# Weighing the heads' values ahead of the next query and key projection in an attention step

## The chip, the core and the metric

The kernel runs on one core of a Trainium2 chip. The metric is the device time of one execution in microseconds (us); lower is better. The core has five engines with a queue each: TensorE (PE, with its weight loads shown apart as PEld), VectorE (DVE), ScalarE (ACT), GpSimd (POOL) and SyncE (SP), which here only issues transfers. Each works through its queue in order and meets the others by semaphores.

## What is computed

A decoder layer on x of 8 x 256 x 256 in float32: causal self-attention with 16 heads of 64, a normalisation, three rounds of a slot attention with a GRU cell against a context of 120 rows, a normalisation, and a mixture of 8 experts of which each token takes 2, with a shared expert, and a last normalisation. The change lies in the first part alone:

```python
q = (x @ Wq).reshape(N, S, HEADS, HEAD_DIM).transpose(0, 2, 1, 3)
k = (x @ Wk).reshape(N, S, HEADS, HEAD_DIM).transpose(0, 2, 1, 3)
v = (x @ Wv).reshape(N, S, HEADS, HEAD_DIM).transpose(0, 2, 1, 3)
logits = jnp.einsum('nhid,nhjd->nhij', q, k) * scale
causal = 1000000000.0 * (jnp.tril(jnp.ones((S, S), dtype=logits.dtype)) - 1.0)
logits = logits + causal[None, None, :, :]
attn = jax.nn.softmax(logits, axis=-1)
out = jnp.einsum('nhij,nhjd->nhid', attn, v)
out = out.transpose(0, 2, 1, 3).reshape(N, S, HEADS * HEAD_DIM)
return out @ Wo + bo
...
x = _layernorm(x + _L0_attn_ref(x, ...), axis=-1)
x = _layernorm(x + _L0_xattn_ref(x, ctx_1024, ...), axis=-1)
x = _layernorm(x + _L0_ffn_ref(x, ...), axis=-1)
```

## The kernel before

The attention works on 64 items. An item is one batch (of 8) and one pair of heads (of 8). Since every matrix of a projection is held as two float16 parts, high and low, a projected tile is three products for each of two chunks of the model dimension (`split_matmuls`, L31): six matmuls for the queries and six for the keys of an item.

The items are software-pipelined over the loop `for j in range(FIRST, LAST + 1)`, which stands once in the program of each engine, written out by hand. What TensorE does in step j, in this order: `turn_prob(j - 1)` transposes the probabilities of item j-1 (L589), `scores(j + 1)` makes the scores of the two heads (L618, each head on one half of the array's rows, into banks 2 and 3), `project_qk(j + 2)` projects queries and keys (L31, tiles `wqkv` and `xT`, into bank 0), and `weigh_values(j - 1)` multiplies the turned probabilities with the values (L628, each head on one half of the array's columns, into the last quarter of banks 4 and 5). Then follows, in odd steps, `project_v(j + 1)` (L31), and in even steps from 4 on a share of the output projection (L31, tiles `wo` and `oT`). In many steps there are also transposes of a later input (L578), preparations for the next stage (`prep_tensor`), or transposes of finished rows.

The other engines in step j:

- ScalarE copies the second head's turned probabilities out of PSUM (L738), makes the high half of a piece of the experts' weights (L477), the first head's exponentials of item j+1 (L721), the queries of j+2 (L728), the high half of the heads of j-1 (`heads_high`, L745), the keys of j+2 (L731), the second head's exponentials, and in early steps high halves of attention weights (L711).
- VectorE copies the first head's turned probabilities (L823), makes the reciprocal sums (L816), low halves of weight pieces (L487), masks and maxima of the scores of j+1 (L809), values out of PSUM (L835), the low half of the heads of j-1 (`heads_low`, L829), and behind that, by step, a batch's output with its statistics (L844, L848, L853, L855), the low half of an input (L787), low halves of attention weights (L796), and more pieces (L487).
- GpSimd multiplies the probabilities by the reciprocal sums (L542).

The waits that matter: `turn_prob(m)` waits for the normalised probabilities and for both halves of the heads of item m-1, since they share a bank. `weigh_values(m)` waits for both copies of the turned probabilities (`pT_out`) and for the values. `project_qk(n)` and `scores(n - 1)` wait for the queries and keys of item n-1 to be out of bank 0. Each bank and each tile `pT` exists once, so that the copies of item m also wait for the weighing of m-1.

SyncE streams the experts' weights in, in pieces, and their split halves out to memory, as VectorE gets done with them.

Of the kernel before, what the change touches and what calls it, by code (L numbers as in the profile page):

```python
# [34 lines left out]
def decoder_layer(nc, a, out):  # L35
# [9 lines left out]
    ITEMS = NB * PAIRS  # L45
# [11 lines left out]
    with top:  # L57
# [256 lines left out]
        def vw_bank(i):  # L314
            return 6 if i == 0 else i - 1 if i < VW_EARLY else i % 4

        def vw_tensor(i):

            b, k = i // 2, i % 2
            before = [q for q in range(i) if vw_bank(q) == vw_bank(i)]  # L320
            if before:
                PE.wait_ge(vw_lo, before[-1] + 1)
            elif i == 0:
                PE.wait_ge(h_out, SHARES_MADE - KEYS)
            elif i == 1:
                PE.wait_ge(qk_out, 2 * ITEMS)
            elif i == 2:
                PE.wait_ge(v_out, ITEMS // 2)
            else:
                PE.wait_ge(masked, 4 * ITEMS)  # L330
            for r in range(DC):
                mm = PE.matmul(ps[0:M, vw_bank(i), 0:3 * P], pnT[:, r, b * M:(b + 1) * M],
                               wb[:, r, k * 3 * P:(k + 1) * 3 * P], start=r == 0, stop=r == DC - 1)
            mm.then_inc(vw_mm, 1)
# [16 lines left out]
        with ExitStack() as c:  # L351
# [57 lines left out]
            def output_share(j):  # L409

                m = j - 4
                return (m // PAIRS, m % PAIRS) if m >= 0 and m % 2 == 0 else None
# [6 lines left out]
            def batch_turned(j):  # L419

                return j // PAIRS + X_EARLY if j % PAIRS == 3 and j // PAIRS + X_EARLY < NB else None
# [4 lines left out]
            def share_at(j):  # L426

                n = (j - 16) // 2
                return n if j % 2 == 0 and 0 <= n < SHARES_MADE else None
# [138 lines left out]
            def attention_tensor():  # L568
# [13 lines left out]
                def turn_prob(m):  # L582
                    PE.wait_ge(normed, 4 * (m + 1))
                    if m >= 1:
                        PE.wait_ge(o_hi, m)
                        PE.wait_ge(o_lo, m)
                    for h in range(2):
                        for blk in range(3):
                            mm = PE.transpose(ps[:, 4 + h, blk * P:blk * P + P],  # L589
                                              prob[m % 3][:, h, blk * P:blk * P + P], ident[:, :])  # L590
                    mm.then_inc(p_turned, 1)

                def project_qk(n):
                    b, cols = n // PAIRS, slice(n % PAIRS * P, n % PAIRS * P + P)
                    if n >= 1:
                        PE.wait_ge(qk_out, 2 * n)
                    if n % PAIRS == 0:
                        PE.wait_ge(x_hi, b + 1)
                        PE.wait_ge(x_lo, b + 1)
                    for k in range(2):  # L600
                        if n == 0:
                            PE.wait_ge(w_lo, k + 1)
                        if n == PAIRS // 2:
                            PE.wait_ge(w_lo, k + 4)
                        w = [[wqkv[h][:, ch, k, cols] for h in range(2)] for ch in range(DC)]
                        x = [[batch_xT(h, b)[:, ch, :] for h in range(2)] for ch in range(DC)]
                        mm = split_matmuls(PE, ps[:, 0, k * S:(k + 1) * S], list(zip(w, x)))
                    mm.then_inc(qk_mm, 1)

                def scores(m):  # L610

                    PE.wait_ge(qk_out, 2 * (m + 1))
                    if m >= 1:
                        PE.wait_ge(masked, 4 * m)
                    for t in range(2):
                        for h in range(2):
                            r = slice(HD * h, HD * h + HD)
                            mm = PE.matmul(ps[:, 2 + h, query_tile(t)], qk[m % 2][r, 0, t * P:t * P + P],  # L618
                                           qk[m % 2][r, 1, 0:(t + 1) * P], start=True, stop=True)
                    mm.then_inc(s_mm, 1)  # L620

                def weigh_values(m):
                    PE.wait_ge(pT_out, 2 * (m + 1))
                    PE.wait_ge(v_out, m // 2 + 1)
                    for t, key, at in ((0, 0, 0), (1, 0, P), (1, 1, 2 * P)):
                        for h in range(2):
                            r = slice(HD * h, HD * h + HD)
                            mm = PE.matmul(ps[r, 4 + t, 384:512], v_sb[m // 2 % 2][:, key, m % 2, r],  # L628
                                           pT[:, h, at:at + P], start=key == 0, stop=key == t, skip_group_check=True)
                    mm.then_inc(o_mm, 1)  # L630

                def project_v(n):

                    b, cols = n // PAIRS, slice(n % PAIRS * P, n % PAIRS * P + 2 * P)
                    if n == 0:
                        PE.wait_ge(w_lo, 3)
                    else:
                        PE.wait_ge(v_out, n // 2)
                    if n == PAIRS // 2:
                        PE.wait_ge(w_lo, 6)  # L640
                    for t in range(S // P):
                        x = [[batch_xT(h, b)[:, ch, t * P:t * P + P] for h in range(2)] for ch in range(DC)]
                        w = [[wqkv[h][:, ch, 2, cols] for h in range(2)] for ch in range(DC)]
                        mm = split_matmuls(PE, ps[:, 1, t * 2 * P:(t + 1) * 2 * P], list(zip(x, w)))
                    mm.then_inc(v_mm, 1)

                def output_projection(b, slot):
                    PE.wait_ge(o_lo, b * PAIRS + slot + 2)
                    PE.wait_ge(o_hi, b * PAIRS + slot + 2)
                    if b == 0:  # L650
                        PE.wait_ge(w_lo, 7 + slot // 2)
                    if b == 0 and slot == 0:
                        PE.wait_ge(x_hi, 1)
                        PE.wait_ge(x_lo, 1)
                    elif b >= 1 and slot == 0:
                        PE.wait_ge(y_added, b)
                    for t in range(2):
                        o = [[oT[h][:, s, t * P:t * P + P] for h in range(2)] for s in (slot, slot + 1)]
                        w = [[wo[h][:, s, :] for h in range(2)] for s in (slot, slot + 1)]
                        mm = split_matmuls(PE, ps[:, 7, t * D:t * D + D], list(zip(o, w)), first=slot == 0 and t == 0,  # L660
                                           last=slot == PAIRS - 2, skip_group_check=True)
                    mm.then_inc(y_mm, 1)
# [4 lines left out]
                for j in range(FIRST, LAST + 1):  # L667
                    if 0 <= j - 1 < ITEMS:
                        turn_prob(j - 1)
                    if 0 <= j + 1 < ITEMS:  # L670
                        scores(j + 1)
                    if j == ITEMS:
                        vw_tensor(1)
                    if j + 2 < ITEMS:
                        project_qk(j + 2)
                    if 0 <= j - 1 < ITEMS:
                        weigh_values(j - 1)
                    if j + 1 < ITEMS and j % 2 == 1:
                        project_v(j + 1)
                    if j == ITEMS - 1:  # L680
                        vw_tensor(0)
                    if output_share(j) is not None:
                        output_projection(*output_share(j))
                    if share_at(j) is not None:
                        turned = min(X_EARLY + (j + 4) // PAIRS, NB)
                        PE.wait_ge(x_hi, turned)
                        PE.wait_ge(x_lo, turned)
                        prep_tensor(share_at(j))
                    if batch_turned(j) is not None:
                        PE.wait_ge(x_hi, batch_turned(j))  # L690
                        PE.wait_ge(x_lo, batch_turned(j))
                        turn_inputs(batch_turned(j))
# [226 lines left out]
            constants_vector()  # L919
            attention_vector()  # L920
            attention_tensor()
            attention_pool()
            nc.all_engine_barrier()
# [1548 lines left out]
```

## Time and profile before

| | us |
|---|---|
| median of 3 runs | 920.73 |
| lowest and highest run | 920.72, 922.23 |
| profiled execution | 920.84 |
| span of the core in it | 919.60 |

| engine | busy us | share of the span | instructions |
|---|---|---|---|
| PE | 888.7 | 97% | 8158 |
| PEld | 674.2 | 73% | 8158 |
| DVE | 637.2 | 69% | 1823 |
| ACT | 551.8 | 60% | 1337 |
| POOL | 348.7 | 38% | 485 |

A matmul's duration in the trace includes the time in which it drains beside the next one. So what a group of matmuls costs is read from its start to the start of the next group, and not from its busy time. The rows of a timeline merge instructions of a kind that follow each other (x12); the time behind the start is that of the merged group. What stands in brackets at the end of a row is the time that the engine sat idle before it, and who ended that.

### The profile page before, as it was taken

Reading aid. Unit: us, or ns where it says so; the run is one execution under the profiler, and the core shown is the slowest. Engines: PE = TensorE matmul, PEld = TensorE weight load, DVE = VectorE, ACT = ScalarE, POOL = GpSimd, SP = SyncE. Lnnn points to the kernel's source line nnn. Section 1 sums busy time; section 2 is a strip of 40 time slices with the busy share of each in tenths; the row PEclk is TensorE's granted clock in tenths of the full one; section 3 lists DMA queues with packets and bytes.
Section 4 is the critical chain, followed back from the end, with each engine's and each line's share of the span. In section 5 each row is a group of like instructions: output and inputs, shape, how many; then the busy total and the mean of one; then the engine's idle time right before and its main releaser. Section 6 shows DMA issues by size and latency. Waiting matters only on the chain. (4 is left out here: it accounts for less than half of the span.)

```text
span 919.6 us, 23720 instructions
## 1 busy us (share of the span) xinstructions
PE 888.7 (97%) x8158; PEld 674.2 (73%) x8158; DVE 637.2 (69%) x1823; ACT 551.8 (60%) x1337; POOL 348.7 (38%) x485
## 2 busy tenths in 40 slices
PE   5999999999999999899999999999999999999996
PEld 4777778777777777666666666676788888887864
DVE  4667777776677766557676777778867767776755
ACT  5778776776676776446555554555455555554555
POOL 2333433342333333224344342444624444444423
PEclk9999999999999999999999999999999999999998
DMA  9743424343324230310000000089542222332226
GB/s 321 186 139 108 161 101 139 111 149 100 125 72 138 93 134 29 44 56 1 1 1 1 2 1 1 1 312 402 173 125 50 51 48 44 51 50 48 43 30 189
DMA packets 61585, 88.09 MB, mean 96 GB/s; under 512 B 17280, under 2 KB 46528, under 8 KB 61344
## 3 DMA queue, kind: packets, MB, share of 16 engines
q1 hardware_dynamic: 53439, 75.52, 24.8%
q0 software_dynamic: 7488, 10.27, 6.9%
q8 instruction: 72, 1.18, 0.5%
q10 hardware_dynamic: 544, 0.79, 0.3%
q14 instruction: 42, 0.34, 0.1%
HBM read 56.00 MB, written 30.56 MB: 94 GB/s over the span
## 5 line engine op out<-in xcount | busy, mean ns | idle before, releaser
L2153 PE MATMUL ps<-slots,e 128*128 128x128 f16 x1872 | 190.1, 219 | 2.1 <-DVE xs L2320 1.9
L542 POOL TENSOR_SCALAR prob<-prob,rden 128x128 f32<-128x128 f32 (+1 forms) x256 | 108.0, 438 | 213.9 <-DVE rden L816 213.9
L2153 PEld LDWEIGHTS ps<-slots,e 128*128 x1872 | 152.5, 97 | 35.7 <-issue 5.0
L721 ACT ACTIVATE prob<-prob,nmx 128x128 f32<-128x128 f32 (+1 forms) x256 | 114.1, 450 | 40.8 <-DVE nmx L809 38.0
L2161 PE MATMUL ps<-e,xT 128*128 x312 | 117.3, 378 | 0.0
L2250 ACT ACTIVATE slots<-slots 128x512 f32<-128x512 f32 x78 | 49.1, 630 | 106.8 <-DVE slots L2304 106.8
L31 PE MATMUL ps<-s,whh 128*128 128x512 f16 x432 | 105.0, 378 | 0.0
L31 PE MATMUL ps<-xT,wqkv 128*128 128x256 f16 x768 | 96.2, 276 | 1.0 <-DVE wqkv L796 1.0
L31 PEld LDWEIGHTS ps<-xT,wqkv 128*128 128x128 f16 x768 | 70.4, 98 | 30.1 <-issue 22.3
L2162 PE MATMUL ps<-e,xT 128*128 x312 | 85.0, 273 | 0.0
L1665 POOL DMA_INDIRECT xg<-rows_x,dst x39 | 40.9, 1049 | 105.5 <-DVE mask L2293 102.1
L809 DVE CUSTOM_DVE_ANT_0 prob<-ps,mask 128x128 f32<-128x128 f32 (+1 forms) x256 | 75.9, 353 | 4.0 <-PE ps L618 4.0
L2309 DVE TENSOR_TENSOR xT<-slots,xT 128x1024 f16<-128x1024 f32 x39 | 47.8, 1225 | 40.0 <-ACT xT L2256 40.0
L2125 POOL DMA_INDIRECT back_y<-xs,dst x39 | 62.2, 1594 | 30.3 <-DMA back_y<-xs,dst 13.4
L2304 DVE SCALAR_TENSOR_TENSOR slots<-ps,b1e 128x512 f32<-128x512 f32 x78 | 53.7, 691 | 26.4 <-PE ps L2153 25.6
L31 PEld LDWEIGHTS ps<-s,whh 128*128 128x128 f16 x432 | 42.2, 101 | 35.5 <-issue 0.2
L823 DVE COPY pT<-ps 128x384 f32<-128x384 f32 x64 | 35.5, 555 | 44.3 <-PE ps L589 44.1
L829 DVE TENSOR_TENSOR oT<-ps,oT 128x256 f16<-128x256 f32 x64 | 27.2, 424 | 51.0 <-ACT oT L745 50.4
L618 PE MATMUL ps<-qk 64*128 64x128 f32 (+1 forms) x512 | 59.3, 350 | 0.7 <-ACT qk L731 0.7
L31 PE MATMUL ps<-an,wqkv 120*128 120x256 f16 x432 | 59.1, 272 | 0.5 <-POOL an L1389 0.5
L31 PEld LDWEIGHTS ps<-an,wqkv 120*128 120x128 f16 x432 | 41.9, 97 | 21.4 <-POOL an L1389 1.0
L1371 POOL TENSOR_TENSOR dl<-slots,nn 128x512 f32<-128x512 f32 x24 | 30.4, 1268 | 70.9 <-ACT nn L1248 70.8
(262 smaller groups left out, 1899.3 us busy)
## 6 DMA issues: line engine op xcount, KB each, us to landing
halves<-parted SPq DMA_DIRECT2D x36, 512.0 KB, 2.9
piece<-in_L_ffn_ew SPq DMA_DIRECT2D x32, 512.0 KB, 4.4
e<-halves SPq DMA_DIRECT2D x16, 1024.0 KB, 15.3
piece<-in_L_ffn_sh_w SPq DMA_DIRECT2D x4, 512.0 KB, 8.8
sw<-halves SPq DMA_DIRECT2D x4, 512.0 KB, 6.3
rows_x<-xs SPq DMA_DIRECT2D x4, 512.0 KB, 6.8
xs<-back_y SPq DMA_DIRECT2D x8, 256.0 KB, 5.2
out<-xs SPq DMA_DIRECT2D x8, 256.0 KB, 2.1
```

The costliest lines, as they stand in the source:

```text
L31: mm = pe.matmul(out, w, x, start=first and n == 0, stop=last and n == len(products) - 1, **kw)
L542: PO.tensor_scalar(prob[m % 3][:, h, r], prob[m % 3][:, h, r], rden[m % 2][:, h, t:t + 1], 1.0, ALU.mult, ALU.mult).then_inc(normed, 1)
L618: mm = PE.matmul(ps[:, 2 + h, query_tile(t)], qk[m % 2][r, 0, t * P:t * P + P], qk[m % 2][r, 1, 0:(t + 1) * P], start=True, stop=True)
L721: SC.activation(p, p, ACT.Exp, bias=nmx[u][:, h, t:t + 1], scale=-1.0, accum_out=den[u][:, h, t:t + 1]).then_inc(exped, 1)
L809: VE.tensor_tensor_reduce(prob[m % 3][:, h, r], ps[:, 2 + h, r], mask[:, r], -1.0, HIGHEST, ALU.add, ALU.min, nmx[m % 2][:, h, t:t + 1]).t ...
L2125: PO.indirect_dma_start(back_y, bass.IndirectOffsetOnAxis(ap=dst[:, i:i + 1], axis=0), yo[i % 2], None, compute_op=ALU.add).then_inc(rows_ ...
L2153: yield PE.matmul(ps[:, 2 * u + q, (k % 4) * P:(k % 4) * P + P], w[ch][h], xgT[u][j][:, ch, :], start=n == 0, stop=n == 3 * DC - 1)
L2161: yield PE.matmul(ps[:, 4 + u, :], he[u][0][:, k, :], w, start=k == 0, stop=False, skip_group_check=True)
L2162: yield PE.matmul(ps[:, 4 + u, 0:D], he[u][1][:, k, :], w[:, 0:D], start=False, stop=k == IC - 1, skip_group_check=True)
L2250: SC.activation(z, z, ACT.Gelu_apprx_tanh).then_inc(U_gelu, 1)
L2304: VE.scalar_tensor_tensor(z, ps[:, 2 * u + q, :].rearrange("p (k t) -> p k t", k=4), 1 / WS, bias, ALU.mult, ALU.add).then_inc(U_bias, 1)
L2309: VE.tensor_tensor(he[i % 2][1], zf.rearrange("p (k t) -> p k t", k=IC), he[i % 2][0], ALU.subtract).then_inc(U_lo, 1)
```

## The change

In TensorE's program of step j the call `weigh_values(j - 1)` moves in front of `project_qk(j + 2)`. Both run together in steps 1 to 61. The programs of the other engines are word for word the same, and no instruction, tile or semaphore is added or taken away.

```diff
@@ -671,10 +671,10 @@
                         scores(j + 1)
                     if j == ITEMS:
                         vw_tensor(1)
+                    if 0 <= j - 1 < ITEMS:
+                        weigh_values(j - 1)
                     if j + 2 < ITEMS:
                         project_qk(j + 2)
-                    if 0 <= j - 1 < ITEMS:
-                        weigh_values(j - 1)
                     if j + 1 < ITEMS and j % 2 == 1:
                         project_v(j + 1)
                     if j == ITEMS - 1:
```

TensorE's queue over one even step, the kernel before, with the semaphores that a group waits for (`ps<-qk` are scores, `ps<-xT,wqkv` the projection of queries and keys, `ps<-pT,v` the weighing, `ps<-wo,oT` the output projection, `ps<-ident,prob` the transposes of probabilities):

```order
511 L618 MATMUL ps<-qk 128x128 [waits masked,qk_out]
512 L618 MATMUL ps<-qk 128x128
513 L618 MATMUL ps<-qk 128x256 x2
514 L31 MATMUL ps<-xT,wqkv 128x256 [waits qk_out]
515 L31 MATMUL ps<-xT,wqkv 128x256 x11
516 L628 MATMUL ps<-pT,v 64x128 [waits v_out,pT_out]
517 L628 MATMUL ps<-pT,v 64x128 x5
518 L31 MATMUL ps<-wo,oT 128x256 [waits o_hi,o_lo]
519 L31 MATMUL ps<-wo,oT 128x256 x11
```

The same place after the change:

```order
511 L618 MATMUL ps<-qk 128x128 [waits masked,qk_out]
512 L618 MATMUL ps<-qk 128x128
513 L618 MATMUL ps<-qk 128x256 x2
514 L628 MATMUL ps<-pT,v 64x128 [waits v_out,pT_out]
515 L628 MATMUL ps<-pT,v 64x128 x5
516 L31 MATMUL ps<-xT,wqkv 128x256 [waits qk_out]
517 L31 MATMUL ps<-xT,wqkv 128x256 x11
518 L31 MATMUL ps<-wo,oT 128x256 [waits o_hi,o_lo]
519 L31 MATMUL ps<-wo,oT 128x256 x11
```

The weighing, with its wait for `pT_out`, now stands directly behind the scores, and the twelve matmuls of the projection stand between it and the step's other projection.

ScalarE's queue over a step, which is the same before and after; the queries (`qk<-ps`, first) wait for the projection, and the heads' high half (`oT<-ps`) stands behind them:

```order
344 L738 COPY pT<-ps 128x384 [waits o_mm,p_turned]
345 L477 ACTIVATE parted<-piece 128x1024 [waits p_out0,p_in0]
346 L721 ACTIVATE prob,den<-prob,nmx 128x128 [waits recip,masked]
347 L721 ACTIVATE prob,den<-prob,nmx 128x256
348 L728 ACTIVATE qk<-ps 128x256 [waits s_mm,qk_mm]
349 L745 CAST oT<-ps 128x256 [waits y_mm,o_mm]
350 L731 ACTIVATE qk<-ps 128x256
351 L721 ACTIVATE prob,den<-prob,nmx 128x128 [waits masked]
352 L721 ACTIVATE prob,den<-prob,nmx 128x256
```

Nothing moved here: what moves is, on TensorE, the end of the projection that row 348 waits for and the end of the weighing that row 349 waits for.

## Rows read from the trace of the kernel before

**Rows 1.** Busy time by engine in the stretch of steps 1 to 61.

```profile
core 0: us, PE busy (x) PEld busy (x) DVE busy (x) ACT busy (x) POOL busy (x), PEclk, DMA share, GB/s
20.64:359.01 338.37, 336.21 (x3162) 260.70 (x3163) 242.94 (x956) 243.72 (x805) 119.59 (x260) 1.00 0.37 122
```

**Rows 2.** Timeline of TensorE, step 55: start us, us, engine, line, tiles.

```profile
321.66 0.82 PE L589 MATMUL ps<-ident,prob 128*128 128x128 f32 x6
322.41 0.93 PE L618 MATMUL ps<-qk 64*128 64x128 f32 x8
323.26 1.48 PE L31 MATMUL ps<-xT,wqkv 128*128 128x256 f16 x12
324.68 0.88 PE L628 MATMUL ps<-pT,v 128*64 128x128 f32 x12
325.49 1.48 PE L31 MATMUL ps<-wqkv,xT 128*128 128x256 f16 x12
326.81 0.27 PE L589 MATMUL ps<-ident,prob 128*128 128x128 f32 x1
```

**Rows 3.** Timeline of the other engines in step 55, and the projection's weight loads.

```profile
322.51 0.56 DVE L823 COPY pT<-ps 128x384 f32<-128x384 f32 x1 [1.00 <-PE ps L589]
...
323.26 1.21 PEld L31 LDWEIGHTS ps<-xT,wqkv 128*128 128x128 f16 x12 [0.33 <-issue]
...
324.95 0.36 ACT L728 ACTIVATE qk<-ps 128x256 f32<-128x256 f32 x1
...
325.60 0.37 ACT L745 CAST oT<-ps 128x256 f16<-128x256 f32 x1 [0.29 <-PE ps L628]
...
326.00 0.42 DVE L829 TENSOR_TENSOR oT<-ps,oT 128x256 f16<-128x256 f32 x1 [1.42 <-ACT oT L745]
```

**Rows 4.** Timeline of TensorE, step 62, without a projection of queries and keys.

```profile
359.76 0.93 PE L618 MATMUL ps<-qk 64*128 64x128 f32 x8
360.62 0.88 PE L628 MATMUL ps<-pT,v 128*64 128x128 f32 x12
```

**Rows 5.** Timeline of step 63, where weighing waits for VectorE's copy.

```profile
364.14 0.56 DVE L823 COPY pT<-ps 128x384 f32<-128x384 f32 x1 [1.03 <-PE ps L589]
...
364.76 0.88 PE L628 MATMUL ps<-pT,v 128*64 128x128 f32 x12 [0.65 <-DVE pT L823]
```

**Rows 6.** Timeline around late copies: steps 1, 6, 36 and 60.

```profile
22.31 1.48 PE L31 MATMUL ps<-xT,wqkv 128*128 128x256 f16 x12
22.82 0.55 DVE L823 COPY pT<-ps 128x384 f32<-128x384 f32 x1
22.93 0.46 ACT L738 COPY pT<-ps 128x384 f32<-128x384 f32 x1
...
47.24 0.82 PE L589 MATMUL ps<-ident,prob 128*128 128x128 f32 x6
...
49.39 0.55 DVE L823 COPY pT<-ps 128x384 f32<-128x384 f32 x1
...
207.93 0.42 DVE L829 TENSOR_TENSOR oT<-ps,oT 128x256 f16<-128x256 f32 x1 [0.79 <-ACT oT L745]
...
210.74 0.55 DVE L823 COPY pT<-ps 128x384 f32<-128x384 f32 x1
210.78 1.48 PE L31 MATMUL ps<-xT,wqkv 128*128 128x256 f16 x12
...
347.48 0.42 DVE L829 TENSOR_TENSOR oT<-ps,oT 128x256 f16<-128x256 f32 x1 [1.43 <-ACT oT L745]
...
349.68 0.56 DVE L823 COPY pT<-ps 128x384 f32<-128x384 f32 x1
```

**Rows 7.** Timeline of step 1: queries to the next step's transposes and scores.

```profile
24.91 0.36 ACT L728 ACTIVATE qk<-ps 128x256 f32<-128x256 f32 x1
...
25.56 0.42 DVE L829 TENSOR_TENSOR oT<-ps,oT 128x256 f16<-128x256 f32 x1 [1.02 <-ACT oT L745]
...
26.13 0.85 PE L589 MATMUL ps<-ident,prob 128*128 128x128 f32 x6
26.91 0.93 PE L618 MATMUL ps<-qk 64*128 64x128 f32 x8
```

## The prediction

> **What bounds the kernel now.** I read the stretch sums first, then the waits, then single steps in order of time. In the 338.37 us in which all 61 changed steps lie, TensorE is busy 336.21 us at a granted clock of 1.00; VectorE has 242.94, ScalarE 243.72 us of work [rows 1]. TensorE's own order and cost set this stage. I number a step by its loop index j: it turns the probabilities of item j-1, makes the scores of j+1, projects j+2, weighs the values of j-1.
>
> Step 55 [rows 2]: six transposes start at 321.66, scores 322.41, projection 323.26, weighing 324.68, value projection 325.49, and the next step at 326.81. From start to start: 0.75, 0.85, 1.42, 0.81, 1.32, together 5.15 us. Beside it [rows 3], VectorE's copy of the turned probabilities ends at 322.51 + 0.56 = 323.07, the queries leave PSUM at 324.95, the heads' high half at 325.60, and the low half ends at 326.00 + 0.42 = 326.42, or 4.76 to 4.77 us into the step. Steps that also turn inputs or prepare weights are longer, 5.59 us being usual.
>
> **What the order removes.** A projection of twelve matmuls takes 1.42 us when weighing follows, and 1.32 when transposes follow (325.49 to 326.81): the array drains before it changes to another form of tile. The first projection weight load of rows 3 stood 0.33 us idle, although the previous weights had long been loaded. Now the two projections, same form, stand together, so the first costs 1.32. Weighing costs 0.81 before whichever projection. Scores followed directly by weighing are not in a usual step, but step 62 has them: 359.76 to 360.62, 0.86 us [rows 4], the same as the 0.85 before a projection. So 0.10 us is gained per step; 61 steps (1 to 61) give 6.2 us of TensorE time. I bound the scores-to-weighing change by 0.85 and 0.90 (0.81 plus one more drain of 0.10), and take 0.86, since its row is the very transition.
>
> Here the Trainium skill speaks against a gain. "TensorE: Matmul & The Clock Gate", section "Part 2: What happens when you issue a matmul", has the queue pull a weight load ahead of running matmuls into the background weights. The trace shows that inside a group, but not across a change of form, where the load waited 0.33 us. By that rule alone no change of form costs anything and nothing would be gained.
>
> **What the order adds, first wait: turned probabilities.** Weighing could start 1.60 us into a step (when the projection starts now), if both copies are done. VectorE's copy reaches a waiting weighing 0.06 us after its end: 364.14 + 0.56 = 364.70, weighing at 364.76 [rows 5]. In step 55 that makes 323.07 + 0.06 = 323.13 against 323.26: no wait, 0.13 us to spare. But in twelve steps (1, 3, 4, 6, 8, 12, 20, 28, 36, 44, 52, 60) VectorE is late, with a copy from 22.82 (the first) to 349.68 (the last) [rows 6], because it first makes weights' low halves (steps 1 to 8) or adds a batch's projection, its statistics and mostly an input's low half. Today the projection hides that. Copy end plus 0.06 less the projection's start, in the twelve: 1.1 (23.40 by ScalarE's copy against 22.31), 0.7, 0.7, 1.15, 1.15, 0.56, 0.83, 0.56, 0.56, 0.57, 0.41, 0.41, together 8.7 us. The wait holds up, in TensorE's queue, both projections and the next transposes.
>
> **Second wait: the heads' eviction.** On ScalarE the order is unchanged: queries, heads' high half, keys, second head's exponentials. The queries need the projection, which now ends 0.8 us later: in step 55 weighing starts at 323.27, projection at 324.08, ends at 325.56; queries at 325.60 instead of 324.95. The weighed heads, though finished early, stand behind them. From a queries start to the next step's transposes, where each follows directly: 24.91, low half at 25.56 + 0.42, transposes at 26.13, so 1.22 us [rows 7]. Hence the next step can't start before 326.82. TensorE alone could start it at 326.71. So **a short step becomes 5.17 us, not 5.05**, against 5.15 now; and a step that starts after such a wait pays 0.03 more before its scores (26.13 to 26.91 is 0.78, against 0.75). A short step thus costs +0.05. In a long step the added work (0.43 us or more) stands before the transposes and covers the wait: −0.10.
>
> The low half now ends 5.02 us into a step instead of 4.77 (326.82 − 0.15). What VectorE does behind it, and its next copy, starts 0.25 later; the next step starts 0.10 earlier if the step is long. So the late copies become later still, by 0.23 to 0.36 us, before the wait is counted.
>
> **Worked, late steps.** Step 36: the low half before it ends at 208.35 (step 35 started 4.77 earlier, 203.58), the copy starts 2.39 later [rows 6]. Now: 203.58 + 5.02 + 2.39 = 210.99, ends 211.55, weighing 211.61; step 36 starts at 203.58 + 5.49 = 209.07 and could weigh at 210.67. Wait 0.93, less 0.10 gained: +0.82. Steps 28 and 44 are alike; 20 has 0.27 more in front: +1.09. Step 12 ends with the heads' wait: weighing 2.53 into the step, projection's end 2.53 + 0.81 + 1.48 = 4.82, + 0.05 + 1.22 = 6.09, against 5.21: +0.88. Step 60: low half's end 347.90, copy 1.78 later, at the old step's 6.55; new 5.02 + 1.78 + 0.56 + 0.06 = 7.42, could weigh at 5.17 + 1.60 = 6.77: wait 0.65, net +0.53; 52 alike. Step 6: copy ends 2.70 into the step (49.94 less 47.24); its chain runs through ScalarE's keys, 0.25 later: 2.93, weighing 2.99, + 0.81 + 1.48 + 0.05 + 1.22 = 6.55, against 5.80 now: +0.75; 8 alike. By the same steps 1: +0.83, 2: +0.22 (it has no second projection; its heads' chain alone sets it, 5.17 against 4.95), 3: +0.58, 4: +0.78, and 11: +0.05 (copy slightly late).
>
> **The sum.** 26 short steps × 0.05 = +1.3. 21 long ones × −0.10 = −2.2. The other 14: 0.83 + 0.22 + 0.58 + 0.78 + 2 × 0.75 + 0.05 + 0.88 + 1.09 + 3 × 0.82 + 2 × 0.53 = +9.5. Together **+8.6 us**. The traced execution took 920.84 (span 919.60), 0.11 above the median; 929.4 there, **929.3 us** as a median. Later stages wait for TensorE's end of this one, their instructions are unchanged, and I cost them at nothing; the transfers of the split weights follow VectorE, but the DMA engines are busy only 0.37 of the stretch [rows 1]. Idle time of TensorE up to 1.1 us goes with a clock of 1.00 in the stretch above, so I cost the clock at nothing too.
>
> **Rivals.**
> A. The heads' chain gives way (later queries cost nothing, VectorE catches up in its idle time): then only the twelve waits count, 8.7 − 6.2 = +2.5, 923.3 us. For it: VectorE is idle 28% of the stretch. Against: that idle time lies ahead of the low half, not behind it, where the late work is.
> B. Faster: the 0.10 us per step is all that stays. The place is the same copy; it decides when the waits in the twelve steps fall under 6.2 us in sum, which needs the copies to come 0.2 us earlier on average; if all go, 920.8 − 6.2 = 914.6. For it: in the other steps the copy has time to spare. Against: nothing moves VectorE's late work forward.
> C. Gain and waits cancel, or weighing is held as long as it was: 920.7. Against: TensorE's order is really changed.
> D. No form change is saved. Where TensorE itself sets the step (21 long, 7 late ones: 20, 28, 36, 44, 52, 60, 3), 0.10 more each: +2.9, 932.2 us. Against: rows 2. This is also what the skill's pull-ahead would leave over from the sum, as worked from the rows.
>
> **How the numbers follow.** Forecast 0.80, A 0.07, B 0.04, C 0.03, D 0.06. The forecast's own range: half the drift of the late copies less (0.15 × 12 = 1.8) and the short steps free (1.3) below, giving 926; 0.05 per step for the unseen transition (3.0) above, giving 932.3. I widen to 925 to 932.5, which takes in D. Below 0.2% (1.8 us) a measurement of this kernel can't tell a change; slower by more: 0.80 + 0.06 + 0.07 = 0.93, within 0.03, faster 0.04.
>
> **What would show it.** Right: scores, then weighing after 0.86, projection after 0.81, second projection after 1.32; short steps of 5.17 to 5.20, whose transposes wait for VectorE's low half; about twelve waits of weighing for VectorE's copy, 0.6 to 1.4 us each, some 12 us in sum; the stage 8 to 9 us longer and everything behind it as long as before. Wrong: if short steps shrink to 5.05, the eviction chain was mis-sized; if the late waits stay at 0.4 to 1.15, the drift was; if weighing starts 1 us or more behind scores in usual steps, the transition was.

## The result

| | before | after |
|---|---|---|
| median of the runs beside each other, us | 921.48 | 931.62 |
| lowest and highest, us | 920.72, 922.45 | 931.28, 931.91 |
| profiled execution: span, us | 919.60 | 930.20 |

The change makes the kernel slower by 1.1%: the ratio is 1.0114, 95% interval 1.0101 to 1.0127. A second set of runs of the same kernel gave 1.0121 (1.0102 to 1.0140).

Weighing always means the product of the turned probabilities with the values (L628), and the stage is steps 1 to 61. First the stretch from the start of step 1 to the start of step 62, which is [rows 1] of the kernel after:

```profile
core 0: us, PE busy (x) PEld busy (x) DVE busy (x) ACT busy (x) POOL busy (x), PEclk, DMA share, GB/s
21.76:369.27 347.51, 335.14 (x3164) 264.46 (x3163) 242.69 (x956) 244.57 (x806) 119.52 (x260) 1.00 0.37 118
```

347.51 us against 338.37: the stage is 9.14 us longer, while the busy time of each of TensorE, VectorE, ScalarE and GpSimd differs by 1.1 us at most. Who waited for whom, the whole list for TensorE in steps 1 to 61 (engine, line, what was waited for: us in total, times, longest), first before, then after:

```profile
PE ps L589 <- DVE oT L829: 2.0, 3, 1.0
PE ps L589 <- POOL prob L542: 0.3, 1, 0.3
```

```profile
PE ps L628 <- DVE pT L823: 9.8, 11, 1.3
PE ps L589 <- DVE oT L829: 1.3, 1, 1.3
PE ps L628 <- ACT pT L738: 1.3, 1, 1.3
```

The weighing never waited before; now it waits in twelve steps, eleven times for VectorE's copy and once for ScalarE's, 11.1 us in sum. These lists count only what stands beyond the modelled ends of the matmuls. Read from the starts instead, weighing begins later than the 1.6 us into the step at which it could, by 12.2 us over the twelve steps together.

Step 55 of the kernel after, the counterpart of [rows 2, 3]:

```profile
331.38 0.82 PE L589 MATMUL ps<-ident,prob 128*128 128x128 f32 x6
...
332.13 0.93 PE L618 MATMUL ps<-qk 64*128 64x128 f32 x8
332.24 0.56 DVE L823 COPY pT<-ps 128x384 f32<-128x384 f32 x1 [0.63 <-PE ps L589]
...
332.99 0.88 PE L628 MATMUL ps<-pT,v 128*64 128x128 f32 x12
...
333.80 1.49 PE L31 MATMUL ps<-xT,wqkv 128*128 128x256 f16 x12
...
335.12 1.47 PE L31 MATMUL ps<-wqkv,xT 128*128 128x256 f16 x12
...
335.32 0.38 ACT L728 ACTIVATE qk<-ps 128x256 f32<-128x256 f32 x1 [0.54 <-PE ps L31]
335.60 0.37 ACT L745 CAST oT<-ps 128x256 f16<-128x256 f32 x1
...
336.00 0.42 DVE L829 TENSOR_TENSOR oT<-ps,oT 128x256 f16<-128x256 f32 x1 [1.69 <-ACT oT L745]
...
336.57 0.84 PE L589 MATMUL ps<-ident,prob 128*128 128x128 f32 x6
```

From start to start: 0.75, 0.86, 0.81, 1.32, 1.45, together 5.19 us. The first projection has lost its 0.10 us; the last group is 1.45 long although its matmuls need 1.32, because the transposes wait for the low half of the heads, which ends at 336.42. The queries start at 335.32, 0.54 us after ScalarE ran out of work, and the heads' high half only behind them.

Steps 35 and 36, the counterpart of [rows 6]: the heads' low half in VectorE's queue, what stands behind it, then the late copy.

```profile
216.20 0.43 DVE L829 TENSOR_TENSOR oT<-ps,oT 128x256 f16<-128x256 f32 x1 [1.06 <-ACT oT L745]
...
216.54 0.68 DVE L844 SCALAR_TENSOR_TENSOR xs<-ps,xs 128x512 f32<-128x512 f32 x1
...
217.07 0.82 PE L589 MATMUL ps<-ident,prob 128*128 128x128 f32 x6
...
218.41 0.68 DVE L787 TENSOR_TENSOR xT<-ps,xT 128x512 f16<-128x512 f32 x1
...
219.01 0.54 DVE L823 COPY pT<-ps 128x384 f32<-128x384 f32 x1
...
219.61 0.44 PE L628 MATMUL ps<-pT,v 128*64 128x128 f32 x4 [0.86 <-DVE pT L823]
```

The copy starts 1.94 us into the step (1.57 before), and weighing 2.54 instead of the 1.60 at which it could: 0.94 us.

### The profile page after: what moved, and what is told of

It reads as the page before. It is cut to its first block and busy times, and to the rows that moved or that the text cites. A ratio compares the mean times of both kernels' runs of the same rounds, so it can differ in the third digit from the quotient of the medians.

```text
span 930.2 us, 23720 instructions
## 1 busy us (share of the span) xinstructions
PE 889.3 (96%) x8158; PEld 679.0 (73%) x8158; DVE 636.9 (68%) x1823; ACT 552.7 (59%) x1337; POOL 348.8 (37%) x485
## 5 line engine op out<-in xcount | busy, mean ns | idle before, releaser
L31 PEld LDWEIGHTS ps<-xT,wqkv 128*128 128x128 f16 x768 | 71.0, 99 | 20.6 <-issue 12.3
L628 PE MATMUL ps<-pT,v 128*64 128x128 f32 x768 | 56.1, 281 | 11.7 <-DVE pT L823 10.4
L628 PEld LDWEIGHTS ps<-pT,v 128*64 128x64 f32 x768 | 40.6, 136 | 33.9 <-DVE pT L823 32.3
```

The source lines that it names most:

```text
L31: mm = pe.matmul(out, w, x, start=first and n == 0, stop=last and n == len(products) - 1, **kw)
```

## The experiments

The lengths of steps below are differences between the starts of the transposes of one step and of the next, in the profiled execution, always against the kernel before. "Short" are the usual steps of 5.15 to 5.18 us, "long" those that also turn inputs or prepare weights. By kind of step, in us:

| kernel | 26 short | 21 long | the other 14 | stage |
|---|---|---|---|---|
| forecast | +1.3 | -2.2 | +9.5 | +8.6 |
| the change | +1.0 | -1.8 | +9.9 | +9.14 |

The expectations of the step lengths came out better than those of the whole time: the medians of experiments 1, 2, 3, 4, 6 and 8 lie above their expected ranges, by 0.3 to 2.1 us. The stage came out 0.4, 0.9 and 0.6 us above what was expected in experiments 3, 4 and 6, and within 0.2 us in 1, 2 and 8; what the traces show outside it stands in the next section.

### 1. The new order in all steps but the twelve

```diff
+                    if 0 <= j - 1 < ITEMS and j not in (1, 3, 4, 6, 8, 12, 20, 28, 36, 44, 52, 60):
+                        weigh_values(j - 1)
                     if j + 2 < ITEMS:
                         project_qk(j + 2)
-                    if 0 <= j - 1 < ITEMS:
+                    if 0 <= j - 1 < ITEMS and not (j not in (1, 3, 4, 6, 8, 12, 20, 28, 36, 44, 52, 60)):
                         weigh_values(j - 1)
```

The diff is against the kernel before.

> Weighing stands ahead of the projection in 49 of the 61 steps and behind it in the twelve with late copies (1, 3, 4, 6, 8, 12, 20, 28, 36, 44, 52, 60). Theory (the loss is the wait for late copies): short steps stay at 5.19 us, long ones at 5.48 to 5.51, step 2 at 5.21, and the twelve fall back to about their old lengths, with 0.1 to 0.4 us left in steps 4, 6, 8, 12 and 20 since their copies come later: +0.5 us over the kernel before in all, 921.3 to 922. Rival (the order costs something in every step, by a dearer change of tile form or by the queries coming later): 49/61 of the loss stays, +7 to +8 us, 928 to 929.

Measured: 922.86 us, ratio 1.0014 (1.0004 to 1.0025), stage +0.66 us. Steps 1, 3, 4, 36 and 44 are as before to 3 ns, 28 is 0.02, 52 and 60 are 0.03 longer; 6 and 8 are 0.24 longer, 20 is 0.26 and 12 is 0.37 longer. So 8.5 of the 9.14 us go when twelve of 61 steps get their old order. In the other 49 the new order saves 0.5 us together, so it has no price of its own there. Expected were +0.5 us and at most 922 us in all.

### 2. The new order in the twelve alone

```diff
+                    if 0 <= j - 1 < ITEMS and j in (1, 3, 4, 6, 8, 12, 20, 28, 36, 44, 52, 60):
+                        weigh_values(j - 1)
                     if j + 2 < ITEMS:
                         project_qk(j + 2)
-                    if 0 <= j - 1 < ITEMS:
+                    if 0 <= j - 1 < ITEMS and not (j in (1, 3, 4, 6, 8, 12, 20, 28, 36, 44, 52, 60)):
                         weigh_values(j - 1)
```

The diff is against the kernel before.

> The other part alone: weighing ahead of the projection in the twelve steps with late copies only. Theory: each waits for its copy as it came before, without the extra 0.2 to 0.4 us of drift, since the steps ahead of it have the old order: copy end plus 0.06 us at 2.17 us into steps 28, 36, 44 instead of 2.54. In steps 28, 36, 44 +0.46, 52 and 60 +0.31, 20 +0.73, 12 +0.5, 6 and 8 +0.5, 1 +0.8, 3 +0.6, 4 +0.8: +6.5 us in all, 927 to 928. With e1's +0.5 that leaves 2 us of the stage's 9.2 to the two parts together. Rival (each late step costs the same with or without the others changed): +9 us, 930. Rival (cost in every step): 12/61 of it, +2, 923.

Measured: 929.06 us, ratio 1.0084 (1.0066 to 1.0102), stage +6.61 us. Steps 28, 36, 44: +0.46 each, their copies ending 2.11 us into the step as before; 52 and 60 +0.31, 20 +0.72, 12, 6 and 8 +0.53 to 0.54, 1 +0.90, 3 +0.58, 4 +0.83. The waits alone give this much. TensorE's list of waits for copies in this kernel; 0.7 us and one of the twelve times in its first row are the wait in step 63, which the kernel before has too [rows 5]:

```profile
PE ps L628 <- DVE pT L825: 7.8, 12, 1.1
PE ps L628 <- ACT pT L740: 1.1, 1, 1.1
```

With the 0.66 of experiment 1 this makes 7.27; the last 1.87 us of the change come only when both parts are there, because the new order in the step ahead ends VectorE's low half 0.27 us later and step 35 itself 0.10 us earlier. So the copy starts 1.94 us into step 36 and not 1.57, and this 0.37 us is what separates +0.46 from +0.83.

### 3. ScalarE's order alone

```diff
+                    if 0 <= j - 1 < ITEMS:
+                        heads_high(j - 1)
                     if j + 2 < ITEMS:
                         queries(j + 2)
-                    if 0 <= j - 1 < ITEMS:
-                        heads_high(j - 1)
```

The diff is against the kernel before.

> The kernel before, with ScalarE's order changed alone: in a step the heads' high half stands ahead of the queries. The weighing ends late there, so the heads can't leave PSUM earlier, and the queries come 0.9 us later but still before the next scores. Theory: usual steps stay at 5.15 and 5.59 us; steps 1, 4, 6, 8 and 12, which end with the wait for the heads' low half, lose 0.1 to 0.26 us each: -0.7 us, 920 to 921. Rival (late queries cost time by themselves, through the second exponentials and the next copy): 0.1 us or more in every step, +6 us or more.

Measured: 921.28 us, ratio 0.9998 (0.9988 to 1.0009), stage -0.30 us. Usual steps are unchanged to 2 ns. Steps 1 and 12 gained 0.20 and 0.06, but 4, 6 and 8 nothing: there the copy came 0.27 us later (2.97 instead of 2.70 us into steps 6 and 8), since it hangs on the keys, which start 0.28 us later, and on ScalarE's weights behind them, and ate the gain. I had overrated this one: expected were -0.7 us. The queries start 0.92 us later in a usual step (4.21 instead of 3.29 us into step 55), and the step is as long as before: late queries cost nothing by themselves.

### 4. The change with ScalarE's heads ahead of the queries

The edit is that of experiment 3, made to the change.

> The change, and with it ScalarE's heads' high half ahead of the queries in every step. Theory (short steps are held by the eviction that stands behind the queries): short steps go from 5.19 to 5.04 us, long ones stay at 5.48, VectorE's low half ends near 4.1 us into the step instead of 5.04, so that the drift of the late copies is gone and their waits fall to 0.4 to 1.15 us, in steps 52 and 60 to nothing: -1.6 us against the kernel before, 919 to 920. Rival (the low half is late for another reason, VectorE's own work): short steps stay at 5.15 or more, and the time above 928.

Measured: 922.09 us, ratio 1.0001 (0.9990 to 1.0011), stage -0.69 us, against +9.14 without this edit. Step 56 of it, TensorE with the eviction of the heads:

```profile
328.54 1.49 PE L31 MATMUL ps<-xT,wqkv 128*128 128x256 f16 x12
...
329.42 0.34 ACT L745 CAST oT<-ps 128x256 f16<-128x256 f32 x1
...
329.80 0.42 DVE L829 TENSOR_TENSOR oT<-ps,oT 128x256 f16<-128x256 f32 x1
...
330.06 0.38 ACT L728 ACTIVATE qk<-ps 128x256 f32<-128x256 f32 x1 [0.29 <-PE ps L31]
```

The high half starts while the projection still runs, 0.64 us ahead of the queries, and the low half is done 0.16 us after these have started. The short steps are now 5.04 us (step 2 is 4.25), all long ones 0.106 us shorter than before. This shows both parts of the second wait: it held the short steps, and it fed the drift. In step 36 the copy ends 1.97 us into the step instead of 2.48, in step 60 at 1.41, without a wait. Step 3 went against me: +1.23 us, where the change alone costs +0.58. Step 2 had become 0.70 us shorter, but the copy of step 3 stayed where it was in time, and so ends 2.92 us into step 3 instead of 2.26. I put that down to ScalarE's chain ahead of it, which no experiment moved. Step 52 too stayed at +0.27. Against a step 3 as in the change and a step 52 without a wait, the two are 1.0 us longer, which is why the stage gained 0.7 and not 1.6 us.

### 5. One piece of VectorE's late work behind the copy

```diff
+                    if batch_turned(j - 1) is not None:
+                        inputs_low(batch_turned(j - 1))
                     if 0 <= j < ITEMS and j % 2 == 0:
                         values_out(j)
...
-                    if batch_turned(j) is not None:
-                        inputs_low(batch_turned(j))
```

The diff is against the kernel after.

> The change, with one piece of VectorE's work moved: the low half of a turned input (0.68 us, six times, at the end of steps 3, 11, 19, 27, 35, 43) goes behind the masks of the next step, and so behind the copy of the turned probabilities. Theory: in steps 4, 12, 20, 28, 36, 44 the copy comes 0.6 us earlier (its end 1.87 instead of 2.48 us into steps 28, 36, 44), weighing starts 0.6 us earlier, and each step is 0.6 us shorter; all others as in the change: -3.7 us against the change, stage +5.5 against before, 926.5 to 928. Rival (the copy waits for something else there): no change, 931.

Measured: 927.55 us, ratio 1.0073 (1.0055 to 1.0091), stage +5.25 us, 3.9 less than the change. Each of the six steps fell by 0.59 to 0.60 us, and nothing else changed but step 1. Step 36:

```profile
212.81 0.82 PE L589 MATMUL ps<-ident,prob 128*128 128x128 f32 x6
...
213.55 0.93 PE L618 MATMUL ps<-qk 64*128 64x128 f32 x8
...
214.14 0.56 DVE L823 COPY pT<-ps 128x384 f32<-128x384 f32 x1
...
214.75 0.88 PE L628 MATMUL ps<-pT,v 128*64 128x128 f32 x12 [0.27 <-DVE pT L823]
...
215.56 1.49 PE L31 MATMUL ps<-xT,wqkv 128*128 128x256 f16 x12
...
216.12 0.69 DVE L787 TENSOR_TENSOR xT<-ps,xT 128x512 f16<-128x512 f32 x1
```

0.68 us of work taken from in front of the copy brought weighing 0.59 us forward. So the wait is for VectorE's queue, as told.

### 6. Both orders new in the 49 steps, both old in the twelve

The edit of experiment 1, and `heads_high` ahead of `queries` in the same 49 steps.

> Both remedies: weighing ahead of the projection, and ScalarE's heads' high half ahead of the queries, in the 49 steps without a late copy; the twelve others in the old order. Theory: 48 steps lose 0.106 us, step 2 0.7 us, the twelve stay within 0.1 us of their old lengths: stage -5.6 us, 915 to 916. Rival (TensorE gives the time back in the old steps, whose transposes or copies come late): -2 us or less.

Measured: 917.16 us, ratio 0.9959 (0.9946 to 0.9972), stage -4.98 us. 48 steps lost 0.106 us each as expected and step 2 lost 0.67; step 4 became 0.59 longer, again behind the shortened step 2. The twelve steps in the old order are 0.8 us longer together, which is why -5.6 us was not reached. In experiment 8, with the low half of the input out of the way, step 4 is only 0.08 us longer.

### 7. The change once more

> The change itself once more, for the microseconds that its stage doesn't explain: the stage of steps 1 to 61 was 9.2 us longer and the medians lay 10.1 apart. The first transposes started at 20.64 us in the profiled execution of before, 21.76 in that of the change, and 20.0 to 21.9 in four others, whatever their order. Theory (the start varies with the first loads, independently of the order): a ratio of 1.010 or a little less, stage +9.2 again, with another start. Rival (the change delays the start or the later stages): start at 21.7 or later again, and again 10 us.

Measured: 933.13 us, ratio 1.0121 (1.0102 to 1.0140), stage +9.22 us, start of step 1 at 21.69 us. I expected a ratio of 1.010 or a little less and another start, and got 1.0121 and the same late start; the next section says what the traces show of it.

### 8. All remedies, in 55 steps

New order of TensorE and ScalarE in steps 1 to 61 but 1, 3, 4, 6, 8 and 52, and the edit of experiment 5.

> All together: weighing and heads first in 55 steps, old order in steps 1, 3, 4, 6, 8 and 52, and the low half of a turned input behind the masks as in e5. Theory: steps 12, 20, 28, 36, 44 and 60 have their copy at 1.41 us and lose 0.11 us (12: 0.17) instead of keeping their old length; stage -6.2 us, 914.5 to 915.5. Rival (the moved low half now delays the heads' low half and with it the next transposes): steps 12, 20, 28, 36, 44 at or over their old lengths, no better than e6.

Measured: 915.97 us, ratio 0.9941 (0.9929 to 0.9953), stage -6.12 us. Steps 20, 28, 36, 44 and 60 lost 0.106 us each, step 12 0.17. The low half moved behind the masks costs nothing, because the heads' low half still ends 4.45 us into the step, 0.6 us or more before the next transposes. This is the fastest version, 0.6% below the kernel before. Step 36 of it on TensorE, with no wait left (0.86 us from scores to weighing):

```profile
206.88 0.82 PE L589 MATMUL ps<-ident,prob 128*128 128x128 f32 x6
207.62 0.93 PE L618 MATMUL ps<-qk 64*128 64x128 f32 x8
208.48 0.88 PE L628 MATMUL ps<-pT,v 128*64 128x128 f32 x12
209.29 1.48 PE L31 MATMUL ps<-xT,wqkv 128*128 128x256 f16 x12
```

## Why the prediction was right, and what it missed

Forecast were 929.3 us in a range of 925 to 932.5, and 931.62 were measured. The stage, for which alone the sum has terms, is 9.14 us longer against the forecast 8.6. In the spans of the profiled executions 2.0 us are missing from the forecast (930.2 against 919.6 + 8.6): 0.54 in the stage, 1.12 before it and 0.32 behind it. That the median fell inside the range is in part luck: the second set of the same kernel has 933.13, which lies outside.

**The change of tile form.** Right to 10 ns (the sum writes 0.10 us per step and reckons 6.2 for 61 steps and 2.2 for 21, which is the 0.106 that came out). Scores to weighing is 0.86 us in step 55 as it was in step 62 of before [rows 4], weighing to projection 0.81, and the first of two projections 1.32. The saving per step is 0.106 us in experiment 4, where nothing else holds the usual steps. Weight loads pulled ahead across a change of form, as rival D has it, are not seen in any trace here. That the array drains in the 0.10 us is the prediction's reading; the rows show the pause and the late load.

**The first wait.** Right. The twelve steps named are the twelve that wait, by 0.54 to 1.28 us each. Steps 28, 36 and 44 came out at +0.83 (forecast +0.82), 60 and 52 at +0.54 (+0.53), 20 at +1.09 (+1.09), 6 and 8 at +0.77 (+0.75), 12 at +0.91 (+0.88), 3 at +0.58 (+0.58), 4 at +0.83 (+0.78). Experiment 2 showed what they cost alone (6.6 us), experiment 5 that it is VectorE's queue in front of the copy. Rival A, the waits without drift, gave +2.5; experiments 1 and 2 show the drift to be worth 1.9 us beyond the two parts. Rival B needed copies that come earlier by themselves; experiments 5 and 8 had to move work to get them. Rival C fell with the stage itself, 9.14 us longer. TensorE's longest idle time in the stage was 1.29 us, and the granted clock stayed at 1.00, so the clock was rightly put at nothing there.

**The second wait.** Right in kind and nearly in size: a short step is 5.19 where I had 5.17, the queries-to-heads pair taking 0.28 us instead of 0.26 when the queries are what ScalarE waits for. Short steps cost +1.0 and long ones -1.8 where I wrote +1.3 and -2.2; the two differ by how the 0.03 us after a wait is shared out, and together are 0.2 us off. What I had not seen is how much hangs on it. Moving the eviction in experiment 4 gives back 9.8 us: 3.9 in the 26 short steps, 0.5 in the long ones and 5.5 in the other 14, where the same late low half feeds the drift and holds steps 1, 2, 4, 6, 8 and 12. Rival A had priced a chain that gives way at 6 us (+2.5 instead of +8.6).

**Step 1**, the only mis-sized term of weight: +1.17 against +0.83. Weighing waited for ScalarE's copy, which ended 3.03 us into the step (2.76 before). It goes with the start of the kernel and not with the order: that copy ended at 2.75 to 2.76 us in the five executions that start early and at 3.03 to 3.18 in the five that start late, among them experiments 1, 3 and 8 with the old order in step 1. In experiments 2 and 5, which start early, the same step cost +0.90, and in the late second run of the change +1.32. The forecast took this wait at 1.1 us and left out the 0.06 us from the copy's end to weighing, most of what lies between 0.83 and 0.90.

**Outside the stage** I had put nothing. Of the 10.6 us between the two spans, 9.1 are the stage, 1.1 lie before step 1 and 0.3 behind step 61. The 1.1 us arise in the first 20 us, where the code is the same. The projections of the first loop steps, the kernel before and after:

```profile
14.46 0.93 PE L618 MATMUL ps<-qk 64*128 64x128 f32 x8 [0.75 <-ACT qk L731]
15.32 1.48 PE L31 MATMUL ps<-xT,wqkv 128*128 128x256 f16 x12
16.64 1.47 PE L31 MATMUL ps<-wqkv,xT 128*128 128x256 f16 x12
```

```profile
13.99 1.65 PE L618 MATMUL ps<-qk 64*128 64x128 f32 x8 [0.75 <-ACT qk L731]
15.58 2.61 PE L31 MATMUL ps<-xT,wqkv 128*128 128x256 f16 x12
18.02 1.47 PE L31 MATMUL ps<-wqkv,xT 128*128 128x256 f16 x12
```

The same twelve matmuls took 2.61 us instead of 1.48. In each trace the record of the granted clock begins with full speed at a certain time, and the matmuls run at half their later speed up to that time: 13.83 us in the kernel before, 17.92 in the kernel after. Nothing is recorded ahead of it, so a mean of 1.00 for those first microseconds tells nothing. Step 1 started at 19.8 to 20.6 us in the five executions whose record begins at 12.4 to 13.8, and at 21.7 to 21.9 in the five in which it begins at 17.9 to 18.4. Both profiles of the change are among the late ones; but so are experiments 1, 3 and 8, and experiments 2, 4 and 5, which have the new order of TensorE in step 1 as well, are among the early. Whether the change has a part in it stays open.

Behind the stage there is a second such place. In four executions (experiments 4 to 7) the granted clock falls for a while some 19 us after step 64 begins, and in the other six it does not. The second run of the change, in this stretch, and twelve matmuls in it:

```profile
core 0: us, PE busy (x) PEld busy (x) DVE busy (x) ACT busy (x) POOL busy (x), PEclk, DMA share, GB/s
397.25:400.65 3.40, 3.40 (x20) 3.25 (x18) 0.76 (x4) 0.60 (x1) 1.02 (x1) 0.50 0.85 202
```

```profile
397.61 2.77 PE L31 MATMUL ps<-s,kq 128*120 128x256 f16 x12
```

The first run of the change, the same stretch and the same matmuls:

```profile
397.25:400.65 3.40, 3.22 (x28) 2.32 (x26) 1.83 (x10) 1.01 (x3) 1.02 (x1) 1.00 0.85 203
```

```profile
397.43 1.47 PE L31 MATMUL ps<-s,kq 128*120 128x256 f16 x12
```

This makes the stretch from step 62 to the end 562.5 us instead of 560.9, for one and the same kernel. So the two profiled executions of the change lie 10.6 and 12.2 us above that of before: 9.1 and 9.2 us are the stage, 1.1 each the start, and 0.3 and 1.9 lie behind the stage. The medians are 10.1 and 12.4 us apart; the executions that were not profiled have no trace, so how often each of the two places was slow in them isn't shown.

## What to carry to other kernels

An order that saves pipeline changes on the busiest engine puts a consumer closer to its producer: list, step by step, when the slower engines deliver, and not only in the usual step, since here twelve unusual ones cost 9.7 us where 47 usual ones gave 0.7. When a producer is moved forward, move its eviction too: behind another instruction in a queue, the result leaves no sooner, and everything queued behind that eviction comes later. Switching the order only where the data is there, moving the eviction together with its producer, and taking one piece of late work out of the copy's way turned a loss of 1.1% into a gain of 0.6%.

## What the runs showed of the hardware

Changing between tiles of 128 x 128 and fp32 tiles of 64 rows or 64 columns cost TensorE about 0.1 us each time, in all ten profiled executions. Matmuls of a projection start 0.109 us apart, and so does the first of the next group of the same form; a first matmul of 64 columns starts 0.201 to 0.209 us behind a projection's last, wherever no wait comes on top. The steps repeat to 2 or 3 ns between executions and kernels when their waits are the same, so that single steps can be compared where whole runs differ by one or two microseconds. TensorE ran its matmuls at half their later speed until the record of a full granted clock begins, at 12.4 to 13.8 us in five executions and at 17.9 to 18.4 in the other five. From the start of step 64 to the end, the kernels took 551.6 to 552.2 us in six executions and 553.2 to 553.5 in the four with a granted clock of 0.50 (1.2 GHz) near its beginning, whatever the order in the attention. In the 10 us ahead of the fall TensorE had been busy 7.64 us, with idle times of 1.17 and 1.19 us; in the first run of the change it had done the same (7.63 us, the same two idle times), and the clock stayed at 1.00.
